# Two batches' shared expert in the tail of attention, fixed expert slots with a table of places, and rows kept on chip

## The reference

```
x += transformer layer (masked self attention, cross attention with ctx, ReLU FFN 1024; 16 heads)
x += int8-quantised 256x256 linear layer of layernorm(x)
x += cross attention with ctx of layernorm(x)
t  = layernorm(x)
logits = t @ router_w.T                      # 16 experts
top_vals, top_idx = top_k(logits, 2); gates = sigmoid(top_vals)
moe    = sum over the 2 chosen experts of gate * (silu(t@Wg_e) * (t@Wu_e)) @ Wd_e      # 256 -> 256 -> 256
shared = (silu(t @ sg.T) * (t @ su.T)) @ sd.T                                        # 256 -> 512 -> 256
x += moe + shared
```

## Time and profile before

| what | us |
|---|---|
| runs (3) | 1541.53, 1547.13, 1552.13 |
| median | 1547.13 |
| time of the profiled execution | 1535.08 |
| its span, first to last instruction | 1533.3 |
| mean granted TensorE clock, share of 2.4 GHz | 0.913 |

### The profile page before, as it was taken

How to read it: one execution, slowest core, us unless ns; L and a number is a source line. 1 busy time by engine, 2 the same in 40 slices (tenths; PEclk the granted TensorE clock), 3 DMA queues, 4 the chain that set the end, 5 groups by cost and what they waited for, 6 DMA issues and landing times. The chain is left out here.

```text
span 1533.3 us, 17810 instructions
## 1 busy us (share of the span) xinstructions
PE 1291.2 (84%) x5544; PEld 562.0 (37%) x5544; DVE 929.4 (61%) x2123; ACT 671.0 (44%) x1243; POOL 466.3 (30%) x728
## 2 busy tenths in 40 slices
PE   5787878878788889988988988988889848999991
PEld 2221322322323233443442443443333224656661
DVE  5799989899885665456455555558667322233333
ACT  1255545455454556445445545535546521112220
POOL 4341633322212323243343343232301004413341
PEclk9598988999899999989999988998989678999996
DMA  7642422424432542221221221222331129722225
GB/s 229 197 131 71 130 77 76 131 56 147 119 92 86 138 125 56 91 69 35 83 77 35 83 76 35 83 68 85 104 89 37 43 73 353 243 71 84 79 64 165
DMA packets 130703, 156.69 MB, mean 102 GB/s; under 512 B 15534, under 2 KB 106162, under 8 KB 130355
## 3 DMA queue, kind: packets, MB, share of 16 engines
q1 hardware_dynamic: 118067, 134.53, 30.0%
q10 hardware_dynamic: 8704, 12.58, 2.6%
q0 software_dynamic: 3840, 8.43, 1.5%
HBM read 93.92 MB, written 63.05 MB: 102 GB/s over the span
## 5 line engine op out<-in xcount | busy, mean ns | idle before, releaser
L1077 DVE TENSOR_REDUCE Mx<-bank 128x1 f32<-128x512 f32 x512 | 341.3, 685 | 304.7 <-PE bank L843 301.4
L750 ACT ACTIVATE prob<-bank 128x512 f32<-128x512 f32 x512 | 290.0, 593 | 253.5 <-PE bank L860 251.8
L860 PE MATMUL bank<-QS,KS 99*128 99x512 bf16 x768 | 315.1, 412 | 68.1 <-ACT prob L750 29.9
L843 PE MATMUL bank<-KS,QS 96*128 96x512 bf16 x768 | 319.2, 416 | 60.1 <-DVE Mx L1074 29.8
L750 ACT ACTIVATE prob<-prob 128x512 f32<-128x512 f32 x256 | 160.6, 629 | 178.5 <-DVE prob L1088 176.8
L873 PE MATMUL bank<-prob,V 128*17 128x512 f32 x1536 | 227.6, 668 | 0.7 <-ACT prob L750 0.7
L860 PEld LDWEIGHTS bank<-QS,KS 99*128 99x128 bf16 x768 | 76.1, 100 | 296.8 <-ACT prob L750 140.2
L843 PEld LDWEIGHTS bank<-KS,QS 96*128 96x128 bf16 x768 | 77.0, 100 | 282.1 <-DVE Mx L1074 104.8
L597 POOL TENSOR_SCALAR MR<-neg 16x128 bf16<-16x128 f32 x48 | 13.8, 288 | 318.5 <-ACT neg L724 318.4
L1088 DVE TENSOR_TENSOR prob<-bank,ff_h 128x512 f32<-128x512 f32 x128 | 87.5, 684 | 16.7 <-PE bank L860 16.3
L1088 DVE TENSOR_TENSOR prob<-bank,mask 128x512 f32<-128x512 f32 x128 | 87.7, 685 | 13.0 <-PE bank L860 12.8
(11 more groups left out here) (157 smaller groups left out, 1727.9 us busy)
## 6 DMA issues: line engine op xcount, KB each, us to landing
stack_scr<-parts SPq DMA_DIRECT2D x48, 384.0 KB, 2.6
QS<-stack_scr SPq DMA_DIRECT2D x48, 384.0 KB, 4.1
KS<-stack_scr SPq DMA_DIRECT2D x48, 384.0 KB, 5.0
stack_scr<-parts SPq DMA_DIRECT2D x48, 256.0 KB, 2.9
w_gu<-in_gate_up ACTq DMA_DIRECT2D x16, 512.0 KB, 5.5
disp<-zero SPq DMA_DIRECT2D x2, 3096.0 KB, 15.4
xr<-disp SPq DMA_DIRECT2D x48, 129.0 KB, 2.0
stack_scr<-parts SPq DMA_DIRECT2D x48, 128.0 KB, 2.8
```

What stands on the lines that cost most here:

```text
L750: act.activation(prob[:, U % NP_, j, :], src, ACT.Exp, scale=CAST).then_inc(exp_done, 1)
L843: pe.matmul(bankS[i % NS][:, :], QS[0:STACK, v, qt * P:(qt + 1) * P], KS[0:STACK, v, :], start=True, stop=True).then_inc(s_full, 1)
L860: pe.matmul(bankT[e % NT][:, :], KS[0:ROWS, h, kt * P:(kt + 1) * P], QS[0:ROWS, h, :], start=True, stop=True).then_inc(t_full, 1)
L1077: dve.tensor_reduce(dst, b, AX.X, ALU.max).then_inc(s_read, 1)
```

## The change

1. **Shared expert of batches 0 and 1 in attention.** `put_shared` adds operations to the list, with last = 207. Gate and up products of batch 0 stand in steps 199, 201, 203, 205, its down products in 207 and 208; those of batch 1 in 211, 212, 213, 215 and 216. They use the three job banks. SiLU is made without its own table: ACT computes exp(-g), POOL adds one (`plus_one`), DVE takes the reciprocal of 128x512 and multiplies twice (`hidden`). The turn, logits, rank and route of the last batch come one step later (213, 214, 215, 216). Experts then has only batches 2 and 3 to do, from `hT_last` and weights already on chip.
2. **Fixed slots.** Expert e owns slots e*2048 onward, so a token's slot is known at `route`. Only a tag (place in `y_tok`, gate; 8 bytes) is scattered into `tag_scr`: 8 indirect DMAs a batch, for batches 0 to 2 within attention (`dispatch`, two in each of four steps), for batch 3 at the start of experts. `tag_scr` is filled beforehand by one 256 KB DMA; the two fills of `disp` are gone.
3. **A table of places.** In experts, when all tags have landed, one indirect DMA fetches 48 rows of tags (one for each tile), PE turns them (after the second pair of batch 3), DVE makes `home`, `token` and `gate`. POOL then gathers each tile's 128 rows from `t_scr` with an indirect DMA, eight ahead, between the scatters to `y_tok`.
4. **Rows stay on chip.** `acc`, `identf`, `tags`, `slot`, `mask0` (with the shared weights) and two `hT` last through both parts. The DRAM copies of the residual, of t transposed and of the routes are gone with their loads.
5. The experts' weights are issued by SP in one run at the start of experts. `y_tok` has all first choices, then all second, so that a final read has two rows of 1 KB for each token instead of one of 2 KB.

```diff
+def put_shared(put, early, late, last):
+    def gate_up(p, m, at):
+        put(late, at, ("gate", p, m), ("up", p, m))
+        put(early, at + 1, ("swish", p, m))
+        put(early, at + 1, ("hid", p, m))
+    def down(p, half, at):
+        put(late, at, ("down", p, half, 0), ("down", p, half, 1))
+        put(early, at + 1, ("sadd", p, half))
+    for m in range(HT):
+        gate_up(0, m, last - 8 + 2 * m)
+    down(0, 0, last)
+    down(0, 1, last + 1)
+    gate_up(1, 0, last + 4)
+    gate_up(1, 1, last + 5)
+    gate_up(1, 2, last + 6)
+    gate_up(1, 3, last + 8)
+    down(1, 0, last + 9)
+    down(1, 1, last + 9)
...
+            f = e if n < NB - 1 else e + 1
+            put(late, f + 2, ("turn", p, 6))
+            put(late, f + 3, ("logits", p))
+            put(early, f + 4, ("top", p))
+            put(late, f + 4, ("rank", p))
+            put(early, f + 5, ("route", p))
+            if p < B - 1:
+                for t in range(QT):
+                    put(late, e + 6 + t, ("dispatch", p, t))
-    for i in range(2):
-        put(late, START[4 + i], ("zero", i))
+    put(late, START[4], ("blank", 0))
+    put(late, START[NB - 1] - 10, ("shared", 0))
...
+                def dispatch(p, t):
+                    pool.wait_ge(route_ready[p], 1)
+                    pool.wait_ge(blanked, 16)
+                    for k in range(2):
+                        pool.indirect_dma_start(tag_scr, bass.IndirectOffsetOnAxis(slot[:, p * QT + t, k:k + 1], 0),
+                                                tags[:, p * QT + t, k, :], None).then_inc(tagged, 16)
+                def plus_one(p, m):
+                    i = p * HT + m
+                    pool.wait_ge(swish_done, i + 1)
+                    pool.tensor_scalar(swish[:, i % 2, :], swish[:, i % 2, :], 1.0, 1.0, ALU.mult, ALU.add)\
+                        .then_inc(swish_plus, 1)
...
+                def hidden(p, m):
+                    i = p * HT + m
+                    e = swish[:, i % 2, :]
+                    dve.wait_ge(swish_plus, i + 1)
+                    link(dve.reciprocal(e, e))
+                    left(dve.tensor_tensor(e, bank_of(("gate", p, m))[:, :], e, ALU.mult), ("gate", p, m))
+                    read_done(dve, ("gate", p, m))
+                    left(dve.tensor_tensor(hid[p][:, m, :], bank_of(("up", p, m))[:, :], e, ALU.mult), ("up", p, m))
...
-                sp.wait_ge(scattered, 32 * TT)
-                for s in range(TILES):
-                    if s >= NX:
-                        sp.wait_ge(yt_read, s - NX + 1)
-                        sp.wait_ge(home_ready, s - NX + 1)
-                    sp.dma_start(xr[:, s % NX, :], x_t[s]).then_inc(xr_in[s % NX], 16)
+                for n in range(NE):
+                    sp.dma_start(w_gu[:, n, :, :], gate_up[n].rearrange("(k p) n -> p k n", p=P)).then_inc(w_in, 16)
+                    sp.dma_start(w_dn[:, n, :, :], down[n].rearrange("(k p) n -> p k n", p=P)).then_inc(w_in, 16)
...
+                for t in range(TT - QT, TT):
+                    for k in range(2):
+                        pool.indirect_dma_start(tag_scr, bass.IndirectOffsetOnAxis(slot[:, t, k:k + 1], 0),
+                                                tags[:, t, k, :], None).then_inc(tagged, 16)
...
+                pool.wait_ge(row_ready, 1)
+                pool.wait_ge(tagged, 32 * TT)
+                pool.indirect_dma_start(table[:, :, :].rearrange("s p c -> s (p c)"), None, table_of,
+                                        bass.IndirectOffsetOnAxis(table_row[0:TILES, 0:1], 0),
+                                        bounds_check=NE * SLOTS // P - 1, oob_is_err=False).then_inc(table_in, 16)
+                pool.wait_ge(token_ready, 1)
+                def rows(s):
+                    if s >= NX:
+                        pool.wait_ge(xT_full, s - NX + 1)
+                    pool.indirect_dma_start(xr[:, s % NX, :], None, tokens_of,
+                                            bass.IndirectOffsetOnAxis(token[:, s:s + 1], 0)).then_inc(xr_in[s % NX], 16)
+                for s in range(NX):
+                    rows(s)
                 for s in range(TILES):
-                    pool.wait_ge(xr_in[s % NX], 16 * (s // NX + 1))
+                    pool.wait_ge(yt_read, s + 1)
                     if s >= 2:
                         pool.wait_ge(yt_out[s % 2], 16 * (s // 2))
-                    pool.tensor_scalar(home[:, s % 2:s % 2 + 1], xr[:, s % NX, D:D + 1], -1.0, 2.0 * TT * P,
-                                       ALU.mult, ALU.add).then_inc(home_ready, 1)
...
                                             yt[:, s % 2, :], None, bounds_check=2 * SLOTS - 1,
                                             oob_is_err=False).then_inc(yt_out[s % 2], 16)
+                    if s + NX < TILES:
+                        rows(s + NX)
...
+                def turn_table():
+                    pe.wait_ge(table_in, 16)
+                    pe.wait_ge(y_read, QT)
+                    for i in range(2):
+                        ins = pe.transpose(bank[7][:, i * TILES:(i + 1) * TILES], table[:, :, i],
+                                           identf[0:TILES, 0:TILES])
+                    ins.then_inc(table_turned, 1)
```

More of the change, by code:

```diff
@@ L193, in jobs_made @@
         return [(kind, *at, half) for half in range(2)]
-    if kind in ("col", "v", "out", "ff1", "i8T", "logits", "rank"):
+    if kind in ("col", "v", "out", "ff1", "i8T", "logits", "rank", "gate", "up"):
         return [(kind, *at)]
-    if kind == "ff2":
+    if kind in ("ff2", "down"):
         return [(kind, *at[0:2])] if at[2] == 0 else []
@@ L216, in jobs_read @@
         return "dve", [("ff2", *at)]
+    if kind == "sadd":
+        return "dve", [("down", *at)]
+    if kind == "hid":
+        return "dve", [("gate", *at), ("up", *at)]
     if kind == "minus":
@@ L941, in _ @@
                         tokens(("ff2", *at[0:2]), at[1], ff_h, w_ff2, FT, (at[2],))
+                    elif kind in ("gate", "up"):
+                        read_done(pe, ("turn", p, NORMS - 1, KD - 1))
+                        if at == [0, 0]:
+                            pe.wait_ge(shared_in, 48)
+                        columns((kind, *at), s_gu[:, ("gate", "up").index(kind), :, :], hT[p], at[1])
+                    elif kind == "down":
+                        read_done(pe, ("up", p, HT - 1))
+                        tokens(("down", *at[0:2]), at[1], hid[p], s_dn, HT, (at[2],))
                     elif kind == "i8T":
@@ L1158, in _ @@
                         add("ff2", p, R[p], T[p], at[1])
+                    elif kind == "hid":
+                        hidden(*at)
+                    elif kind == "sadd":
+                        dve.wait_ge(hn_ready[p], NORMS)
+                        add("down", p, R[p], R[p], at[1])
                     elif kind == "i8turned":
@@ new lines, in add_shared @@
+                def add_shared(c):
+                    for t in range(QT):
+                        n = c * QT + t
+                        r = EARLY_SHARED * QT + n
+                        dve.wait_ge(y_full, n + 1)
+                        dve.tensor_tensor(acc[:, r, :], bank[4 + n % 4][:, 0:D], acc[:, r, :], ALU.add)\
+                            .then_inc(y_read, 1)
+                places()
+                for c in range(LATE):
+                    for m in range(HT):
+                        n = c * HT + m
+                        dve.wait_ge(sg_done, n + 1)
+                        dve.tensor_tensor(hid[:, c % 2, m, :], bank[(n % 2) * 2 + 1][:, :], sg[:, n % 2, :],
+                                          ALU.mult).then_inc(hid_done, 1)
+                        if n == 0:
+                            tile_experts()
+                        if c and m == 0:
+                            add_shared(c - 1)
+                        if c and m == 1:
+                            addresses()
@@ L1545, in read_rows @@
+                add_shared(LATE - 1)
                 def read_rows(s):
```

308 lines of the change are left out of this document (143 added, 165 removed).

## The result

| | before | after |
|---|---|---|
| median, us (range, runs) | 1544.46 (1535.68 to 1552.13, 20) | 1551.78 (1546.99 to 1556.77, 20) |
| ratio to before | | 1.0048, 95% interval 1.0034 to 1.0062 |
| profiled execution: span, time | 1533.3, 1535.08 | 1547.9, 1549.61 |

What follows compares the result with a forecast made beforehand. PE was taken to bound experts up to the first tile, a dependent chain the tail of attention. -4 +18 +32 +2 -53 +2 +1 = -2: span 1531, 1545 on the runs' scale; forecast's own range 1535 to 1558, overall 1524 to 1568.

Steps and rivals of the forecast that it cites:

- A: Attention, near 510: without the fills of disp, PE's 4.18 us wait for DMAs of maxima goes; -4 us.
- B: Steps 199 to 210: batch 0's shared products, half clock and bank waits lengthen the stretch; +18 us (+11 to +26).
- Rival 3: Tail of attention: PE at 1.2 GHz all through and banks late, 16 us more, 1561; chance 0.14.
- C: Last output product to next part: batch 1's shared work and 4.1 us reciprocals lengthen the chain; +32 us (+25 to +40).
- Rival 1: Tail of attention: reciprocals near 0.69 us, or PE kept at 2.4 GHz; 11 us less each, both 1528; chance 0.24.
- D: Dispatch and rest of attention: 24 indirect DMAs on POOL delay maxima; +2 us (0 to 5).
- E: Start of experts: only two batches remain, 44.5 us against 97.4, with weights and table hidden; -53 us (-49 to -56).
- rival 4: Start of experts: late transfers, weights at 300 GB/s or late tags holding PE; +10 us, 1555; chance 0.06.
- F: Tile loop: POOL's scatter and gather, 2.6 us together, stay hidden under PE's 3.02 period; +2 us (0 to +28).
- Rival 2: Tile loop: POOL becomes the bound between scatter and gather; +25 us, 1568; chance 0.13.
- G: Final reads: packets of half the size may make the first read a little longer; +1 us (0 to +2).

Runs made afterwards that it cites:

- e5: Changed kernel with the two 3 MB fills put back in steps 72 and 88, into a buffer nothing reads; 1557.07 us, ratio 1.0108 to before.
- e2: Changed kernel with the eight reciprocals replaced by ordinary multiplications of the same shape, so SiLU is not computed; 1533.42 us, ratio 0.9946 to before.
- e3: Changed kernel with SiLU by ScalarE's tanh, without reciprocal or GpSimd addition; 1530.11 us, ratio 0.9931 to before.
- e7: e1 with all 32 tag scatters at the start of experts instead of 24 in attention; 1577.69 us, ratio 1.0266 to before.
- e1: Changed kernel with the index tables and blank table ahead of the eight tag scatters on GpSimd; 1544.63 us, ratio 1.0023 to before.
- c1: Changed kernel with both tanh SiLU and index tables ahead of the tag scatters; 1518.62 us, ratio 0.9875 to before.
- e4: Changed kernel with the early shared expert undone, all four batches in experts again; 1535.92 us, ratio 0.9965 to before.
- c3: c1 with only one batch's shared expert early, placed from the last output product on; 1520.87 us, ratio 0.9879 to before.
- c4: c1 with both early batches' shared expert placed only from the last output product on; 1520.41 us, ratio 0.9829 to before.

## Why the prediction was wrong

The forecast of "within 1%" came true and its range held the time, but its sign and its sum did not: -2 forecast, +14.6 between the two profiles (+12.5 against the mean of both profiles of before), +7.3 between the medians. The difference that I had thought beyond measuring, under 1%, was measured: 0.5%, with an interval of 0.3 to 0.6. By its steps:

- **A, the fills (-4): right in kind, slightly small.** The wait for maxima went with them and comes back with them (e5). The whole effect is about -5, so a part of it is spread over the stage and no single wait shows it. The 4.18 us that I read in the earlier trace rows is of a weight load; the products themselves stood 3.68.
- **B, steps 199 to 210 (+18, measured +30): the term that failed most.** I priced it as 28 us of old work at a better clock (7 less than before), products of 20.6 us and 3.4 more for one pair at half clock, less 0.8 us for each of five groups that fill idle time, and 5 for waits on VectorE. That has TensorE idle 1 us more than before. It was idle 9.2 us more: the stretch from step 199 to the last addition has 36.6 us busy of 43.9 before, 57.6 of 74.0 after. So the step that failed is the overlap: next to nothing was filled, and TensorE's waits for VectorE (mask, ranks, `ff_h`) are 9.8 us, not 5. The other part is the clock: the shared products took 27.4 us (18.3 in L891, 9.1 in L901), where these 33 and 32 instructions would take 21.1 at full clock: 6 us for the clock, not 3.4. And the old work sped up by 4.9 us, not by my 6.9, as the groups of the two largest kinds show (interval B, before and then after; against the second profile of before it is 2.2):

```profile
L873 PE MATMUL bank<-prob,V 128*17 128x512 f32 x72 | 13.7, 847 | 0.7 <-ACT prob L750 0.7
L860 PE MATMUL bank<-QS,KS 99*128 99x512 bf16 x29 | 13.5, 511 | 3.1 <-ACT prob L750 2.9
```

```profile
L891 PE MATMUL bank<-hT,mask 128*128 128x512 f32 x33 | 18.3, 682 | 1.5 <-DVE mask L1219 1.4
L952 PE MATMUL bank<-prob,V 128*17 128x512 f32 x72 | 11.2, 698 | 0.0
L939 PE MATMUL bank<-QS,KS 99*128 99x512 bf16 x29 | 11.1, 417 | 3.1 <-ACT prob L821 2.9
L901 PE MATMUL bank<-mask,ff_h 128*128 128x256 f32 x32 | 9.1, 448 | 4.8 <-DVE ff_h L1221 4.8
```

The wait for ScalarE of 3.1 us in all, which I had meant to fill with pairs, stands unchanged; I take it that the pairs lie at other places of the order than the waits, which no run shows. Without the reciprocals B is 8 us shorter (e2). With the cheap SiLU of e3 it is 63.7, so 21 us of products added 13 to 20, by which price of the old work (51 or 44) one takes. Rival 3 had B at +26; it named the clock and the banks, and both came, but not the clock all through (0.82 granted on the average).
- **C, the last chain (+32, measured +31): right in mechanism, and in size partly by luck**, since the reciprocal takes 3.35 us and not 4.1, which should have taken 3 us off. The clock took them back: the fourth pair needed 6.18 us (3.43 at full clock) and the down products 9.78 (6.91), where I had 3.43 and some 8. The reciprocal's time lies below both figures of the prediction, 4.1 and 4.3, and the measurement decides. My reading of the earlier trace rows left out a slope: from 8 to 16 elements it is 5.6 ns an element, which gives 3.0 us for 512, so the rows allowed 3.0 to 4.7. Rival 1's first half (a kind reciprocal) is worth 11 us of C in e2, 7 in my bounds.
- **D (+2, measured +3.5): in range, the cause not shown.** The interval is 668.5 and 670.8 in the two profiles of before and 670.5 in e7 without the scatters, so 2 us lie within what one kernel differs by.
- **E, start of experts (-53, measured -43): failed by a step that was missing.** I counted the eight scatters as the delay of the table and of the rows, which stood hidden, and did not ask what else was queued behind them on GpSimd: two index tables for which VectorE waits, ahead of the `hid` for which TensorE waits. The price was 5.6 us of wait and 2.9 of half clock behind it. e1 puts them first and gives 6.5 of the 10 us; c1 gives all 8.5 and reaches 45.3, 0.8 from my 44.5. The weights, which I had at 36 us and so hidden by 8, landed after 40.6 to 46.3 us, and in e1 TensorE waited 3.2 us for them: they came at 232 GB/s from 1330 to 1340 with scatters under way, and only then at 374. With four times the scatters e7 has 112 to 175 GB/s from 1320 to 1360, at a DMA share of 0.92 to 1.14, and 344 behind the last of them, so the scatters are what slows the loads. This is the mechanism of rival 4, of which the changed kernel itself shows no cost and e1 2 of its 10 us.
- **F, tile loop (+2, measured -1): right that it stays hidden.** Rival 2, GpSimd as the bound, did not come. It would have needed a start of some 0.8 us before the scatter and the gather both; the gather paid 0.30, and the scatter's 0.8 runs from the end of ScalarE's instruction, beside the gather. By how much the rival missed isn't shown (0.01 to 0.44 us a tile).
- **G (+1, measured +1): in range**, but not to be told from nothing, as it is 24.8 to 26.3 in the twelve profiles of the changed kernel and its variants and 24.7 and 25.4 before.

Sum of the misses: B 12, E 10 and D 1.5, less 3 in A, 3 in F, 1 in C and 2 before the first product of V: +14.5, so -2 became +12.5. The rest between this and the 7.3 of the medians is in executions of which there is no trace. That the kernel before sometimes gets the slower B of 50 us that e4 shows would fit, but no profile shows it, and it stays open.

## What to carry to other kernels

Work moved to where an engine idles must be priced with everything it brings along: here the products were 41 us, and the SiLU made for VectorE that came with them cost 24 us of it in B and C (after against e3), which an algebraic rewrite gives back. When a small instruction is placed behind a row of long ones on the same engine, follow who waits for it through every engine, even if the instruction itself takes 0.1 us; 0.3 us of index tables held TensorE for 5.6, and the lower clock behind the wait took 2.9 more. And move work in halves: here the first half (c3) gave 20 us for 8, the second (c4 against c3) 21 for 24.

## What the runs showed that I had not expected

- The fp32 reciprocal takes 3.35 us for 512 elements a partition, 4.9 times the 0.69 of a plain product of that size; from the small rows the slope had given 3.6 to 4.7, or 3.0 by the last two alone.
- The granted clock stayed at 0.50 for some 20 us in e4 while TensorE was busy 7.0 to 9.4 of each 10 us, in work that another kernel ran at 0.95 to 1.00 while busy 6.8 to 7.8: the same products, B 7 us apart. Why is open.
- The time of an indirect scatter to land, and the load beside it, grow with the number of scatters: 7.1 to 18.2 us for the 32 of e7 beside the weight loads, 5.2 to 8.7 for the eight of e1 beside the same loads.
- GpSimd starts a gather 0.30 us behind a scatter, but the scatter that waits for ScalarE 0.73 behind the gather. Counted from the end of ScalarE's instruction it is 0.81 us, whether GpSimd came free at 1404.08, 0.08 us behind that end, or long before it.
